# One change in three stages of a hybrid model: first convolution tap and decay clip on ScalarE, causal masks of one-head banks inside VectorE's maximum

## The reference, cut to what matters

```python
# mamba: a causal depthwise convolution with D_CONV = 4 taps over 256 inner channels
x_conv = conv_b + sum((xp[:, k:k + l, :] * conv_w[:, k] for k in range(D_CONV)))
x_conv = _silu(x_conv)
# retention: two decays for each of 32 heads, clipped to (0.85, 0.9995)
beta = jnp.clip(jax.nn.sigmoid((x @ Wbeta.T + bbeta).reshape(b, t, NH, M)), BMIN, BMAX)
K = K * bt[..., None] + pk[:, :, None, :]
# last attention: 16 heads of 8 channels, causal
scores = jnp.where(causal, jnp.einsum('bqhd,bkhd->bhqk', Q, K), -jnp.inf)
probs = jax.nn.softmax(scores / sqrt(hd), axis=-1)
```

## Time and profile before

| | us |
|---|---|
| median of 3 runs | 2204.74 |
| lowest and highest run | 2204.45, 2205.43 |
| the profiled execution, its own time | 2204.35 |
| its span | 2202.6 |

### The profile page before, as it was taken

How to read it: one execution, slowest core, us unless ns; L and a number is a source line. 1 busy time by engine, 2 the same in 40 slices (tenths; PEclk the granted TensorE clock), 3 DMA queues, 4 the chain that set the end, 5 groups by cost and what they waited for, 6 DMA issues and landing times. The chain is left out here.

```text
span 2202.6 us, 35939 instructions
## 1 busy us (share of the span) xinstructions
PE 1956.4 (89%) x12434; PEld 1468.8 (67%) x12434; DVE 1684.0 (76%) x5253; ACT 1038.3 (47%) x1617; POOL 491.6 (22%) x556
## 2 busy tenths in 40 slices
PE   5786799998999966673899979999999999989999
PEld 3554699987899823332799955556556556559998
DVE  6997788876888879998788877766766666627887
ACT  3442244433444434442444445665655665554443
POOL 1110100012000022320200024543544544330000
PEclk8998999999999987876899989999999999989999
DMA  3000100000000010000000000000000000000000
GB/s 100 6 5 4 56 1 1 1 1 1 1 1 1 1 40 1 0 1 0 1 1 1 1 1 1 1 1 1 1 1 1 1 1 1 1 1 11 11 8 14
DMA packets 17639, 15.75 MB, mean 7 GB/s; under 512 B 4210, under 2 KB 16178, under 8 KB 16947
## 3 DMA queue, kind: packets, MB, share of 16 engines
q1 hardware_dynamic: 15152, 12.66, 1.8%
q10 hardware_dynamic: 2306, 0.78, 0.2%
HBM read 10.55 MB, written 2.88 MB: 6 GB/s over the span
## 5 line engine op out<-in xcount | busy, mean ns | idle before, releaser
L2284 DVE TENSOR_REDUCE soft_mx<-psum 128x1 f32<-128x512 f32 (+3 forms) x608 | 380.7, 659 | 196.8 <-PE psum L2153 109.3
L2199 ACT ACTIVATE soft_prob<-psum 128x1024 f32<-128x1024 f32 (+3 forms) x384 | 305.1, 813 | 205.9 <-PE psum L2079 204.8
L163 POOL TENSOR_TENSOR norm_rstd<-norm_mv,s_const_minus_half 128x4 f32<-128x4 f32 x64 | 65.2, 1019 | 916.5 <-DVE norm_mv L158 909.6
L2149 PE MATMUL psum<-soft_own,soft_stack 128*128 128x512 f32 (+3 forms) x768 | 250.3, 376 | 15.7 <-DVE soft_mx L2284 13.4
L2079 PE MATMUL psum<-soft_stack,soft_own 128*128 128x512 f32 (+3 forms) x768 | 228.4, 380 | 2.9 <-POOL soft_stack L2056 2.2
L2079 PEld LDWEIGHTS psum<-soft_stack,soft_own 128*128 128x128 f32 x768 | 121.3, 189 | 133.4 <-issue 74.5
L2149 PEld LDWEIGHTS psum<-soft_own,soft_stack 128*128 128x128 f32 x768 | 139.2, 192 | 74.3 <-DVE soft_mx L2284 59.7
L1075 DVE SCALAR_TENSOR_TENSOR x<-psum,ffn1b_cw,x 128x128 f32<-128x128 f32 x512 | 144.2, 344 | 31.3 <-PE psum L949 22.6
L2096 PE MATMUL psum<-soft_prob,soft_v_pad 128*32 128x512 f32 (+3 forms) x1536 | 163.6, 498 | 3.5 <-ACT soft_prob L2199 2.1
L1075 DVE SCALAR_TENSOR_TENSOR x<-psum,ffn0b_cw,x 128x128 f32<-128x128 f32 x512 | 144.2, 344 | 27.1 <-PE psum L949 18.4
L1075 DVE SCALAR_TENSOR_TENSOR x<-psum,ffn0a_cw,x 128x128 f32<-128x128 f32 x512 | 144.2, 344 | 27.1 <-PE psum L949 18.4
(11 more groups left out here) (377 smaller groups left out, 4055.4 us busy)
## 6 DMA issues: line engine op xcount, KB each, us to landing
s_ffn_w<-in_ffn_w SPq DMA_DIRECT2D x4, 1024.0 KB, 7.6
out_x<-x SPq DMA_DIRECT2D x8, 256.0 KB, 2.3
x<-in_x SPq DMA_DIRECT2D x4, 384.0 KB, 7.4
mamba_coef_dram<-mamba_out_coef SPq DMA_DIRECT2D x8, 96.0 KB, 1.6
s_ret_w<-in_ret_w SPq DMA_DIRECT2D x1, 640.0 KB, 3.6
x<-in_x SPq DMA_DIRECT2D x4, 128.0 KB, 3.6
s_ret_cos<-in_ret_cos SPq DMA_DIRECT2D x1, 512.0 KB, 6.8
s_ret_sin<-in_ret_sin SPq DMA_DIRECT2D x1, 512.0 KB, 6.9
```

Source lines behind the costliest of these rows:

```text
L163: self.nc.gpsimd.tensor_tensor(self.rstd[:, :], self.mv[:, :, 1], self.const["minus_half"][:, 0:GT], ALU.pow).then_inc(self.rstd_ready, 1)
L2149: ins = pe.matmul(per_head[:, n, :], stack[:, u % HT, i * P:(i + 1) * P], own[:, u % 3, g, half * BLK:half * BLK + width], start=(n == 0), ...
L2199: nc.scalar.activation(prob[:, done % PROBS, :, low(n):BLK], e_ps[:, n % 2, :, low(n):BLK], ACT.Exp, scale=float(HD) ** -0.5).then_inc(exp ...
L2284: nc.vector.tensor_reduce(mx[:, i, half, heads.start:heads.stop], bank[:, 0:width * len(heads)].rearrange("p (g k) -> p g k", k=width), AX ...
```

## The change

ScalarE makes the first tap of both halves after both copies of `project`, and VectorE's `convolve` starts with the second tap when ScalarE is done. In the retention the clip becomes three ScalarE passes: a Relu in place of the affine step, and two new passes in place over 128x1024; VectorE loses its clip and sets three bias columns at the start. In the last attention the masked jobs with one head lose their mask matmul; VectorE instead runs tensor_tensor_reduce, which adds a row of masks from SBUF, writes the sum back to the PSUM bank and takes the maximum. POOL builds the row of masks (384 columns of zero and the 128 of causal) in the memory of w["sel"] at the stage's start.

```diff
@@ mamba scan, ScalarE: project(a)
                     nc.scalar.copy(xp[:, i, :, CONV - 1:], ring_ps[:, i, :, :]).then_inc(ring_used, 1)
+                if a:
+                    act.wait_ge(xc2_ready, a)
+                for i in range(HALVES):
+                    act.wait_ge(ring_used, RING * a + i + 1)
+                    nc.scalar.activation(cv[:, i, :, :], xp[:, i, :, 0:P], ACT.Identity, scale=w["conv_w"][:, i, 0:1],
+                                         bias=w["conv_b"][:, i:i + 1]).then_inc(tap_done, 1)
                 for i in range(HALVES):
                     act.wait_ge(ring_ready, RING * a + 2 + i + 1)
...
@@ mamba scan, VectorE: convolve(a, i)
-            STEPS, BOUND_STEPS, PREP_STEPS, CONV_STEPS = 5, 2, 13, HALVES * (CONV - 1)
+            STEPS, BOUND_STEPS, PREP_STEPS, CONV_STEPS = 5, 2, 13, HALVES * (CONV - 2)
...
-                link = Chain(dve, conv_link, CONV_STEPS * a + (CONV - 1) * i).link
-                dve.wait_ge(ring_used, RING * a + i + 1)
-                link(nc.vector.tensor_scalar(cv[:, i, :, :], xp[:, i, :, 0:P], w["conv_w"][:, i, 0:1],
-                                             w["conv_b"][:, i:i + 1], ALU.mult, ALU.add))
+                link = Chain(dve, conv_link, CONV_STEPS * a + (CONV - 2) * i).link
+                dve.wait_ge(tap_done, HALVES * a + i + 1)
                 for k in range(1, CONV):
...
@@ retention, ScalarE
             act.wait_ge(weights_ready, 3)
+            act.wait_ge(clip_ready, 3)
...
-                nc.scalar.activation(beta[:, a % 2, :, :], th[:, :, :], ACT.Identity, bias=w["half"][:, :], scale=0.5)\
+                nc.scalar.activation(beta[:, a % 2, :, :], th[:, :, :], ACT.Relu, bias=clip[:, 0:1], scale=0.5)\
                     .then_inc(beta_ready, 1)
+
+            def clip_decays(a):
+                now = beta[:, a % 2, :, :]
+                act.wait_ge(beta_ready, a + 1)
+                nc.scalar.activation(now, now, ACT.Relu, bias=clip[:, 1:2], scale=-1.0).then_inc(narrowed, 1)
+                act.wait_ge(narrowed, a + 1)
+                nc.scalar.activation(now, now, ACT.Identity, bias=clip[:, 2:3], scale=-1.0).then_inc(clipped, 1)
...
             exponentials(0)
+            clip_decays(0)
             copy_x(1)
...
                     exponentials(i + 1)
+                    clip_decays(i + 1)
                 copy_num(i, 0)
...
@@ retention, VectorE
             nc.vector.memset(eps[:, :], DEN_EPS)
+            for i, bias in enumerate((0.5 - BETA_MIN, BETA_MAX - BETA_MIN, BETA_MAX)):
+                nc.vector.memset(clip[:, i:i + 1], bias).then_inc(clip_ready, 1)
             dve.wait_ge(*loaded)
...
             def features(a):
                 p = a % 2
-                dve.wait_ge(beta_ready, a + 1)
-                nc.vector.tensor_scalar(beta[:, p, :, :], beta[:, p, :, :], BETA_MIN, BETA_MAX, ALU.max, ALU.min)\
-                    .then_inc(clipped, 1)
                 dve.wait_ge(exp_done, a + 1)
...
@@ last attention
+        mask_row = w["sel"][:, :, :, :].rearrange("p i k c -> p (i k c)")
+        mask_ready = sem("mask_ready")
...
                     nc.gpsimd.memset(v_pad[:, h, :, :, HD:HD + 1], 1.0).then_inc(ones_set, 1)
+                    if h == 0:
+                        pool.wait_ge(sel_ready, 1)
+                        nc.gpsimd.memset(mask_row[:, 0:BLK - P], 0.0)
+                        nc.gpsimd.tensor_copy(mask_row[:, BLK - P:BLK], w["causal"][:, :]).then_inc(mask_ready, 1)
...
@@ last attention, TensorE: event "m"
-                                        start=(n == 0), stop=half != i // GT)
-                    if half == i // GT:
+                                        start=(n == 0), stop=half != i // GT or len(heads) == 1)
+                    if half == i // GT and len(heads) > 1:
                         ins = pe.matmul(per_head[:, :, width - P:width], ident[:, :],
...
@@ last attention, VectorE: event "m"
                     dve.wait_ge(m_ready, done + 1)
-                    nc.vector.tensor_reduce(mx[:, i, half, heads.start:heads.stop],
-                                            bank[:, 0:width * len(heads)].rearrange("p (g k) -> p g k", k=width),
-                                            AX.X, ALU.max).then_inc(m_done, 1)
+                    if half == i // GT and len(heads) == 1:
+                        if u == 0:
+                            dve.wait_ge(mask_ready, 1)
+                        nc.vector.tensor_tensor_reduce(bank[:, 0:width], bank[:, 0:width], mask_row[:, BLK - width:BLK],
+                                                       1.0, -3.0e38, ALU.add, ALU.max,
+                                                       mx[:, i, half, heads.start:heads.stop]).then_inc(m_done, 1)
+                    else:
+                        nc.vector.tensor_reduce(mx[:, i, half, heads.start:heads.stop],
+                                                bank[:, 0:width * len(heads)].rearrange("p (g k) -> p g k", k=width),
+                                                AX.X, ALU.max).then_inc(m_done, 1)
```

More of the change, by code:

```diff
@@ L288, in mamba_scan @@
         g_ready, gt_ready, u_ready = sem("g_ready"), sem("gt_ready"), sem("u_ready")
+        tap_done = sem("tap_done")
         h_ready, hm_ready, y_ready, y_copied = sem("h_ready"), sem("hm_ready"), sem("y_ready"), sem("y_copied")
@@ L1379, in retention_stage @@
         eps = sb("eps", [P, 1])
+        clip = sb("clip", [P, 3])
         shift = sb("shift", [P, GT])
@@ L1405, in retention_stage @@
         ring_ready, ring_used, tanh_done = sem("ring_ready"), sem("ring_used"), sem("tanh_done")
-        beta_ready, clipped = sem("beta_ready"), sem("clipped")
+        beta_ready, narrowed, clipped, clip_ready = sem("beta_ready"), sem("narrowed"), sem("clipped"), sem("clip_ready")
         mix_ps_ready, mix_tanh_done, mix_ready = sem("mix_ps_ready"), sem("mix_tanh_done"), sem("mix_ready")
```

## The result

The changed kernel takes **2213.91 us** (median of 6 runs, 2211.9 to 2215.23) against 2204.76 for the kernel before (6 runs): ratio 1.0032, 95% interval 1.0022 to 1.0042. That is slower by 9.2 us, where 2203.0 was forecast and the range ended at 2213.0. Two of the nine executions of masks_twice, one of the experiments, took 4700 us, more than twice the others, and no number here counts them.

The account below looks back on a forecast made before the run. The prediction took VectorE to bound the mamba scan and retention, and TensorE, closely followed by VectorE, the last attention. Its terms, 6.3 - 3.6 + 0.4 - 10.0 + 5.2 = -1.7, gave 2203.0 us, range 2195.0 to 2213.0.

Parts of the forecast that it names:

- Mamba tap: Mamba scan: VectorE loses 16 first taps but waits for ScalarE's tap of half 0; net loss of 6.3 us.
- 3 x 1.34 + 5 x 0.45 = +6.3: Mamba: 3 of 8 tiles, copies 1.7 apart, lose 1.34 us each; the other 5 lose 0.45 each.
- stated bound of +10.7: Mamba tap's upper bound in us, if all tiles had their two copies 1.7 apart.
- Retention: Retention: VectorE loses 8 clips of 0.61 us, ScalarE's two new passes hidden in its idle time; gain of 3.6 us.
- 6 x 0.61 = -3.6: Retention: the clip's 0.61 us gained in six blocks; in two, phi waits for ScalarE's exponential anyway.
- Attention's start: Start of last attention: POOL's mask-row building and its wait for ScalarE's selection passes; loss of 0.4 us.
- Masks: Last attention: 256 mask matmuls off TensorE, 15.4 us, share kept 0.65; gain of 10.0, between 0 and 15.4.
- Fused instruction: Last attention: VectorE's fused sum and maximum takes longer, on the path in 87 jobs; loss of 5.2 us.
- d = 0.06: Last attention: extra time in us of one tensor_tensor_reduce over the tensor_reduce it replaces, taken from a one-element memset, 59 ns.
- slower rival: VectorE, last attention: the maximum's second result costs a full small instruction, 0.17 us; 2212.6 us, chance 0.20.
- faster one: VectorE, last attention: the fused instruction takes no longer than the plain maximum; 2197.8 us, chance 0.28.
- third rival: TensorE, last attention: the mask matmuls' saving vanishes in PE's waits for the two banks; 2213.0 us, chance 0.08.

Follow-up runs that it names:

- masks_twice: Kernel before plus only the fused sum and maximum, TensorE's mask matmuls kept so the mask is added twice: 2211.85 us, ratio 1.0030.
- tap_only: Kernel before with only the mamba part, both halves' first taps on ScalarE: 2217.25 us, ratio 1.0053.
- clip_pool: Kernel before with only the retention part, and POOL's addition to x moved ahead, beside VectorE's statistics of z: 2202.39 us, ratio 0.9980.
- pool_only: Kernel before with the clip left on VectorE and only POOL's addition to x moved ahead: 2205.56 us, ratio 1.0002.
- clip_only: Kernel before with only the retention part, the clip moved to ScalarE: 2205.67 us, ratio 1.0003.

## Why the prediction failed

The sign of the sum hung on a balance of five terms, and two of them were wrong. With these two at what their parts measured alone (+12.5 and -0.4) and the other three as predicted, the sum is +7.7, 2212.4.

- **Mamba tap, +6.3, measured +10.4 (+12.5 alone).** The step that failed is the price of a tile by VectorE's own delay alone, "3 x 1.34 + 5 x 0.45 = +6.3", on the ground that "VectorE is the bound". The three reads and TensorE's L402 and L406 behind them were named, and TensorE's later start was put at nothing. TensorE waits 0.95 longer, its clock falls in most tiles, its products grow by up to 1.64 (6.23 - 4.59), and VectorE, taken as the bound with nothing to wait for, waits for them. The wait itself was priced too high as a whole, 6.3 against 3.8, because the tiles with copies 1.7 apart were counted as a fixed share (three of eight before, two in the changed kernel); in a tile as in the earlier trace rows the prediction said +0.45, and the tile with its clock up takes 22.0 in place of 21.65, +0.35. The stated bound of +10.7 was passed by tap_only.
- **Retention, -3.6, measured +1.1 and -0.4 alone.** The step that failed is "6 x 0.61 = -3.6": it asked whether another engine's result was awaited (phi's wait for ScalarE, which is there as said), and not what runs on POOL while VectorE runs earlier. What it met there took the gain back: 4.6 in ten scans of five blocks. With POOL's addition out of the way the clip is worth 3.3 (clip_pool against pool_only), so the term itself was sized well. ScalarE's passes cost nothing, as said.
- **Attention's start, +0.4.** POOL's L163 comes later by the two new instructions, its next addition starts 4.37 after the first pad in place of 3.92, +0.45, and TensorE's first selection matmul 5.78 after its first matmul of the stage in place of 5.37, +0.41. The number is right, in part by luck: no wait for ScalarE's passes shows, and the two instructions take 0.63 (1300.34 to 1300.97) where 0.44 was taken.
- **Masks, -10.0.** Measured -12.1, within the stated 0 to -15.4: the share kept is 12.1 of 15.4, 0.79 where 0.65 was taken.
- **Fused instruction, +5.2.** d = 0.06 was right to the digit, and masks_twice shows +6.2. There is luck in the digit: the row taken as the nearest is a memset busy for 59 ns, and what runs is an accumulator's read busy for 142 ns, of which all but 0.07 lies under the next instruction. The two terms and the start give -4.4 by the prediction, -6.1 in the change. The slower rival (d at 0.17) and the faster one (d of 0) are out. That the third rival's 2213.0 lies near the measured time is chance: its cause, masks without effect, isn't what happened.

The rule of the Trainium skill that the prediction drew on ("VectorE: DVE Perf Modes", section "Two Vector instructions with no wait between them"), an accumulator's output as an instruction of its own, is confirmed: the row is DVE_READ_ACCUMULATOR2_ANT, 142 ns, of which 0.07 shows between one fused instruction and the next.

For the retention the Trainium skill has the rule that was missed: "SBUF — State Buffer", section "Who interferes with whom", says that a VectorE instruction with two inputs in SBUF contends with a GpSimd instruction that reads SBUF, as its second input comes through a read interface that the two share, and that the order of issue decides which of them is held. The trace agrees: the scan takes 2.37 beside POOL's 1.25, and 1.28 without it. On the order the rows decide nothing: the scan begins 0.04 ahead of the addition at 917.02, where it is held, and 0.02 ahead at 885.00, where it holds POOL.

## What to carry to other kernels

Work taken off the busiest engine moves everything behind it to another time, so ask for each later instruction what it will run beside, POOL's passes over SBUF above all. Where a change delays what releases TensorE, price TensorE's longer idle time by rows at both clock levels and not by the delay alone. And a wait placed ahead of other instructions in a queue delays those too: price each of them by who waits for it.

## What the runs showed of the hardware that was not expected

- Three discarded products of 512 columns a tile shortened the kernel by 7.5 us, as they kept the granted clock at 1.00 where it was 0.67.
- VectorE's 2.37 us for a scan of 1.28: held for about the length of one GpSimd addition, with no wait on any semaphore in the rows. Which of the two was held went with the scan's kind in all ten meetings of the changed kernel and clip_only: a scan that starts from a stored state was held (six), one that starts from zero held POOL (four). So the engines' streams meet in SBUF too, and not only at semaphores, as the introduction has it.
- VectorE writing its sum back into the PSUM bank takes 706 ns against 687 for the maximum that writes one value; nearly all of d is the accumulator's read (0.07 from its start to the next start).
- An unedited stage of 67 us scattered by over 3 us between kernels. A total that moves by less than that says nothing of a part; the part's own stage does.
